# DMA scratch cut to 4 KB: three tiles for x, four band buffers from the first group on, eight of 16 blocks on GpSimd, weights loaded by SyncE

## The chip, the cores and the metric

One core of a Trainium2 chip. The metric is device time in microseconds of one execution, lower is better; a kernel's time is the median of its runs. TensorE (PE) multiplies, VectorE (DVE), ScalarE (ACT) and GpSimd (POOL) work on rows of up to 128 partitions, SyncE (SP) only issues DMAs. SBUF is one arena of 128 partitions that the kernel divides by hand.

## The reference

```
x: (16, 192, 32, 32) f32                       # B, C, H, W
w_sym = (w + rot90(w) + rot180(w) + rot270(w)) * 0.25      # w: (192, 1, 7, 7)
x = x + depthwise_conv7x7(layernorm_over_C(x, eps=1e-6), w_sym, pad=3)
t = tokens(x)                                  # (16, 1024, 192)
h = bitlinear(layernorm_over_C(t, eps=1e-5), W1, b1)       # 192 -> 768, sign weights in 5 groups of rows,
h = gelu(h)                                    #   then 8-bit absmax scaling in 5 groups of 3 images
t = t + bitlinear(h, W2, b2)                   # 768 -> 192, the same two steps
return t back as (16, 192, 32, 32)             # image 16 gets zero from bitlinear: x alone
```

## The kernel before, in words

The work has three stages; the change touches the first two and what prepares the third.

Stage one (to about 88 us) takes x in eight pairs of images. SyncE loads pair k in three DMAs (`load_x`, L310 to L314) into a tile `nat[k % 2]` of 12 KB per partition: one of the two tiles lies over the end of `X1` (the place of the last pair), the other at `R`, behind `XN`. TensorE transposes it in eight steps per pair (L958, L959, semaphore `tr1`), so that pixels are on partitions, ScalarE evicts each step into `X1` (`bring`, L469), VectorE takes statistics of it (`stats1`, L685, `merge`), ScalarE the square root (`deviation`, L475), VectorE the factors (`factors1`, L691 and L693, semaphore `nm`). The 16 blocks of a pair (4 image rows of one image each) are then normalised into `XN`, those in `VBLK` by VectorE (L700), the others by ScalarE (L482). `XN` holds channels outermost, so a block's 192 values are written 512 bytes apart.

Meanwhile VectorE builds the convolution's bands: it symmetrises the 7x7 kernels and writes them 32 times, shifted, into `KX`, a tile that was zeroed half by VectorE (L644) and half by GpSimd (L394). `KX` lies in the part of `X1` where pairs 2 to 5 go, so their evictions wait until SyncE has stored its four pieces to the DRAM tensor `kz_d` (L323), one piece ahead of the load of each of the pairs 2 to 5.

Stage two (to about 235 us) is the convolution as banded matrices: 48 groups of 4 channels, 24 matmuls each (L976, semaphore `conv`), after which VectorE adds the group's result to `X1` (L750, `cev`). A group's bands are four DMAs from `kz_d` of 112 KB, each for 32 partitions and with pieces of 896 bytes (`load_bands`, L296): SyncE issues two, ScalarE two (from group 2 on). The space between the bands must be zero; the loads write only the bands, so a buffer is zeroed once, by GpSimd (semaphore `blank`), before its first use. Buffer of group u is `BUFS[u]`: two buffers lie at `R` (behind the whole of stage one's tile), a third lies in `XN` and is used from group 5 (`THIRD`) on, when the channels under it are done, a fourth from group 26 (`FOURTH`). At group 24 (`conv` 24) GpSimd issues ten DMAs for the weights W1 (five of 51 partitions with 2304 bytes each, L409) and W2 (five of 38 partitions with 3072 bytes, L411) into places in `XN`; VectorE sums them from group 28 on, ScalarE takes their signs from group 38 on, TensorE transposes them.

Stage three is the two matrix products with their scaling, over half images; none of its code is changed. Its `normal` (L816 on VectorE, L426 on GpSimd) and GpSimd's `low` (L435) appear in rows below.

The order on each engine is the order in which its program is written; engines meet only at semaphores.

## Time and profile before

| | us |
|---|---|
| median of 3 runs (611.32, 613.7, 615.29) | 613.7 |
| profiled execution, its own time | 617.74 |
| its span, first to last instruction | 615.9 |
| TensorE busy in it | 496.8 (81%) |
| VectorE busy | 467.1 (76%) |
| ScalarE busy | 382.0 (62%) |
| GpSimd busy | 219.7 (36%) |

Busy times are sums over the whole span and say nothing of which engine a stage waits for; the rows below are cut by stage for that. The profile names engines PE, DVE, ACT, POOL, SP; a `q` behind the name is its queue of issued DMAs, and L976 is line 976 of the kernel. Text in brackets behind a timeline row is the idle time of the engine just before it and what ended that.

### The profile page before, as it was taken

What the parts mean: (1) busy time and instruction counts of PE and PEld (TensorE: products, weight loads), DVE (VectorE), ACT (ScalarE), POOL (GpSimd) and SP (SyncE); (2) the same over time, 40 slices, a digit from 0 to 9 for tenths busy, and PEclk for the clock granted to TensorE, in tenths of its full rate; (3) what the DMA queues carried; (4) which work ended last, traced back from release to release, by engine and by line L of the source; (5) the groups of instructions that cost most, each with busy time, mean ns of one, the idle gap of its engine ahead of it and who ended that gap; (6) DMA issues with size and microseconds to landing.
All of it is one profiled execution on the core that took longest, in us unless ns stands there. A gap on an engine that the chain in (4) does not pass through costs nothing.

```text
span 615.9 us, 9847 instructions
## 1 busy us (share of the span) xinstructions
PE 496.8 (81%) x3552; PEld 353.5 (57%) x3552; DVE 467.1 (76%) x1041; ACT 382.0 (62%) x598; POOL 219.7 (36%) x221
## 2 busy tenths in 40 slices
PE   2355527999969996758789989998999999987893
PEld 2255527999969995324335545555555555545562
DVE  7987861222228987996799898799989989699675
ACT  2688950000000353637799989998999898989550
POOL 4000000000400002212076747576666567558450
PEclk9666759999979997979999989999999999999798
DMA  8998325566965646940011000122222423263345
GB/s 223 290 316 248 104 61 150 149 175 169 204 161 150 178 124 250 386 157 1 27 51 53 27 27 0 52 82 74 78 74 77 133 78 101 80 230 104 125 135 178
DMA packets 55280, 81.29 MB, mean 132 GB/s; under 512 B 7361, under 2 KB 39105, under 8 KB 55232
## 3 DMA queue, kind: packets, MB, share of 16 engines
q1 hardware_dynamic: 39616, 68.28, 36.5%
q10 hardware_dynamic: 15136, 11.22, 6.5%
q0 software_dynamic: 480, 1.17, 0.9%
q8 instruction: 28, 0.46, 0.3%
q14 instruction: 20, 0.16, 0.1%
HBM read 53.12 MB, written 27.53 MB: 131 GB/s over the span
## 4 chain that ended last, share of the span: by engine, by line
PE 42%; DVE 22%; ACT 18%; DMA 10%; issue 5%; SPq 3%; ACTq 0%; DVEq 0%
PE bank L976 19%; DMA arena<-x 6%; PE bank L1058 5%; ACT arena L566 5%; DVE am L844 5%; ACT arena L560 4%; DMA arena<-kz_d 3%; PE bank L1026 3%; PE bank L1027 3%; PE bank L1028 3%; PE bank L1068 2%; DVE arena L816 2%; DVE arena L831 2%; ACT arena L482 2%; DVE arena L766 2%
## 5 line engine op out<-in xcount | busy, mean ns | idle before, releaser
L435 POOL TENSOR_TENSOR arena<-arena 128x512 f16<-128x512 f32 x159 | 186.9, 1212 | 120.6 <-DVE arena L831 99.3
L976 PE MATMUL bank<-arena 128*128 128x112 f32 (+1 forms) x1152 | 136.1, 283 | 20.8 <-ACT arena L482 12.6
L560 ACT ACTIVATE arena<-bank,b1s 128x512 f32<-128x512 f32 x180 | 125.1, 703 | 42.2 <-PE bank L1028 41.8
L976 PEld LDWEIGHTS bank<-arena 128*128 128x128 f32 x1152 | 135.0, 199 | 21.7 <-ACT arena L482 12.8
L1058 PE MATMUL bank<-arena 128*128 128x512 f16 x360 | 106.4, 390 | 5.4 <-ACT arena L584 3.6
L566 ACT ACTIVATE arena<-arena,gm 128x1024 f32<-128x1024 f32 x90 | 102.7, 1163 | 1.7 <-DVE gm L866 1.7
L844 DVE TENSOR_REDUCE am<-arena 128x1 f32<-128x3072 f32 x30 | 100.3, 3343 | 3.5 <-ACT arena L560 3.5
L750 DVE TENSOR_TENSOR arena<-bank,arena 128x512 f32<-128x512 f32 x48 | 33.2, 691 | 81.0 <-PE bank L976 80.9
L1026 PE MATMUL bank<-arena 128*128 128x512 f16 x180 | 71.0, 395 | 26.0 <-DVE arena L824 17.7
L497 ACT ACTIVATE arena<-arena,wmean 51x576 f16<-51x576 f32 (+1 forms) x10 | 8.6, 856 | 129.0 <-DVE wmean L724 116.2
L1027 PE MATMUL bank<-arena 128*128 128x512 f16 x180 | 70.6, 392 | 0.0
L1028 PE MATMUL bank<-arena 128*128 128x512 f16 x180 | 70.2, 390 | 0.0
L958 PE MATMUL bank<-identf,arena 128*128 128x128 f32 x128 | 33.4, 365 | 40.9 <-DMA arena<-x 40.9
L1058 PEld LDWEIGHTS bank<-arena 128*128 128x128 f16 x360 | 34.5, 99 | 47.7 <-issue 4.6
L426 POOL TENSOR_SCALAR arena<-arena,VR,SM 128x192 f32<-128x192 f32 x28 | 14.4, 526 | 108.8 <-DVE arena L816 75.7
L816 DVE TENSOR_SCALAR arena<-arena,VR,SM 128x192 f32<-128x192 f32 x92 | 44.1, 539 | 8.4 <-issue 8.2
L1026 PEld LDWEIGHTS bank<-arena 128*128 128x128 f16 x180 | 17.8, 99 | 56.6 <-DVE arena L824 21.3
L958 PEld LDWEIGHTS bank<-identf,arena 128*128 128x128 f32 x128 | 22.7, 194 | 42.8 <-DMA arena<-x 32.6
L831 DVE CAST arena<-arena 128x2048 f16<-128x2048 f32 (+1 forms) x30 | 35.8, 1195 | 13.6 <-ACT arena L566 11.9
L1068 PE MATMUL bank<-arena 128*64 128x256 f16 x720 | 46.1, 276 | 0.0
L1068 PEld LDWEIGHTS bank<-arena 128*64 128x64 f16 x720 | 37.5, 109 | 13.8 <-issue 13.4
L573 ACT ACTIVATE arena<-arena 128x1024 f16<-128x1024 f32 x37 | 39.7, 1072 | 1.7 <-PE bank L1068 1.7
(118 smaller groups left out, 684.9 us busy)
## 6 DMA issues: line engine op xcount, KB each, us to landing
arena<-park_d SPq DMA_DIRECT2D x44, 384.0 KB, 3.6
arena<-kz_d SPq DMA_DIRECT2D x100, 112.0 KB, 2.9
arena<-kz_d ACTq DMA_DIRECT2D x92, 112.0 KB, 3.4
park_d<-arena SPq DMA_DIRECT2D x6, 1536.0 KB, 14.5
arena<-x SPq DMA_DIRECT2D x8, 1024.0 KB, 8.9
out<-arena SPq DMA_DIRECT2D x32, 256.0 KB, 2.0
kz_d<-arena SPq DMA_DIRECT2D x8, 672.0 KB, 11.0
arena<-x SPq DMA_DIRECT2D x16, 256.0 KB, 9.8
```

The lines of the kernel that those rows point to most:

```text
L435: last = pool.tensor_tensor(out=low_half(u, m, m + 1), in0=yslot(u)[:, 2 * m:2 * m + 2, :], in1=hib(u, m, m + 1), op=ALU.subtract)
L560: act.activation(yslot(s)[:, 2 * m:2 * m + 2, :], m1p[c % 2][:, :].rearrange("p (h n) -> p h n", h=2), ACT.Identity, bias=b1s[:, m:m + 1], ...
L566: act.activation(y, y, ACT.Gelu, scale=gm[:, 5:6]).then_inc(gelu, 1)
L816: last = v.tensor_scalar(TN[:, h % 2, jj, :], x1[:, jj, :], VR[:, n:n + 1], SM[:, n:n + 1], ALU.mult, ALU.add)
L844: v.tensor_reduce(am[:, u % GT:u % GT + 1], yslot(u), AX.XY, ALU.max, apply_absolute_value=True).then_inc(amx, 1)
L958: t.transpose(o[:, b, 0:P], nat[k % 2][:, b, cols], identf[:, :])
L976: last = t.matmul(ps[:, :, lo:hi], WB[BUFS[g]][:, 1 - db, c, :], xn[:, :, lo + db:hi + db], start=(db == 0), stop=(db == -1))
L1026: t.matmul(o, W1A[:, fs], TT[:, s % 2, 0, :], start=True, stop=False)
L1027: t.matmul(o, W1M[:, fs], TT[:, s % 2, 1, :], start=False, stop=False)
L1028: t.matmul(o, W1Q[:, fs], TT[:, s % 2, 2, :], start=False, stop=True).then_inc(mm1, 1)
L1058: last = t.matmul(o, W2T[:, m, 0:P], src, start=(i == n == 0), stop=(i == MT - 1 and n == 1))
L1068: last = t.matmul(m2b[e * C1:(e + 1) * C1, 0:QTR], W2T[:, m, P:C], src[:, e, :], start=(m == n == 0), stop=(m == MT - 1 and n == 1))
```

## The change

The scratch that the program sets aside for DMAs described by software goes from its default of 16 KB to 4 KB of each partition; the arena grows by these 3072 words. They are used so:

- x has three tiles: two at `R`, one over the end of `X1`. Loads 0, 1 and 2 are issued at once, load k waits for the transposition of pair k-3. The pieces of `KX` are stored ahead of pairs 3 to 6.
- Four band buffers lie at `R`, over two tiles of x. GpSimd clears the first two once pair 6 is transposed and the last two once pair 7 is. Groups 0 to 3 are loaded whole by SyncE, later ones half by ScalarE.
- GpSimd normalises eight blocks of each pair (`GBLK`), VectorE two, ScalarE six; in the last pair it is four, six and six.
- The weights are loaded by SyncE, one DMA behind the band loads of each of the groups 16 to 25.
- `KX` is zeroed in three shares: the first half by VectorE before all else, the third quarter by ScalarE's copy of zeros, the last by GpSimd.
- `bring` is issued in two halves with `deviation` of the pair before between them, for every pair; VectorE calls `factors1` in the middle of `stats1`.

```diff
@@ -46,7 +46,7 @@
-ARENA = 52480
+ARENA = 55552
 YR, Y2R = 9, 8
...
@@ -56,7 +56,9 @@
-VBLK = {k: (0, 1, 2, 3, 8, 9, 10) if k < PAIRS - 2 else tuple(range(9)) for k in range(PAIRS)}
+VBLK = {k: (0, 8) if k < PAIRS - 1 else (0, 1, 2, 8, 9, 10) for k in range(PAIRS)}
+GBLK = {k: (1, 2, 3, 4, 9, 10, 11, 12) if k < PAIRS - 1 else (3, 4, 11, 12) for k in range(PAIRS)}
+NATS = 3
...
@@ -69,12 +71,8 @@
-THIRD, FOURTH = 5, 26
-BUFS = [(0, 1, 0, 1, 0, 2)[u] if u <= THIRD else (1, 0, 2)[u % 3] if u < FOURTH else (3, 2, 1, 0)[(u - FOURTH) % 4]
-        for u in range(NCG)]
-ROOM = {THIRD: 3, FOURTH: 23}
+BUFS = 4
+ROOM_W = (12, 17)
...
@@ -109,14 +107,13 @@
         PW = 3 * PIX
-        nat = [view(at, PW).rearrange("p (s n) -> p s n", s=3) for at in (XB - 2 * NB * C, R)]
+        nat = [view(at, PW).rearrange("p (s n) -> p s n", s=3) for at in (R, R + PW, XB - 2 * NB * C)]
...
-        spare = XB + WW + WTN + GROUPS * (3 * C + HID)
-        wb_at = [R, R + WW, XB, spare]
-        assert WW <= NN * CG * ROOM[THIRD] and spare + WW <= XB + NN * CG * ROOM[FOURTH]
+        assert 2 * WW == PW
+        wb_at = [R + i * WW for i in range(BUFS)]
         WF = [view(at, WW) for at in wb_at]
...
@@ -288,13 +280,13 @@
-            q.wait_ge(blank, 1 if u < THIRD else 2 if u < FOURTH else 3)
-            if user_before(u) >= 0:
-                q.wait_ge(conv, user_before(u) + 1)
+            q.wait_ge(blank, 1 if u % BUFS < 2 else 2)
+            if u >= BUFS:
+                q.wait_ge(conv, u - BUFS + 1)
             for r in rows:
-                dst = WF[BUFS[u]][r * W:(r + 1) * W].rearrange("p (c q) -> p c q", c=CG)
+                dst = WF[u % BUFS][r * W:(r + 1) * W].rearrange("p (c q) -> p c q", c=CG)
                 q.dma_start(dst[:, :, (r + 1) * W:(r + 1 + KS) * W], kz_d[u].rearrange("w (c q) -> w c q", c=CG)) \
-                    .then_inc(ld_wb[BUFS[u]], 16)
+                    .then_inc(ld_wb[u % BUFS], 16)
...
@@ -308,28 +300,36 @@
             def load_x(k):
-                t = nat[k % 2]
-                sp.dma_start(t[:, 0:2, :], x[2 * k:2 * k + 2, 0:P, :].rearrange("b c n -> c b n")).then_inc(ld_x[k % 2], 16)
+                t = nat[k % NATS]
+                sp.dma_start(t[:, 0:2, :], x[2 * k:2 * k + 2, 0:P, :].rearrange("b c n -> c b n")).then_inc(ld_x[k % NATS], 16)
                 for e in range(2):
-                    sp.dma_start(t[e * C1:(e + 1) * C1, 2, :], x[2 * k + e, P:C, :]).then_inc(ld_x[k % 2], 16)
-            load_x(0)
-            load_x(1)
-            for k in range(2, PAIRS):
-                i = k - 2
-                if i < W // KP:
-                    sp.wait_ge(ker_step, 8 + KP * (i + 1))
+                    sp.dma_start(t[e * C1:(e + 1) * C1, 2, :], x[2 * k + e, P:C, :]).then_inc(ld_x[k % NATS], 16)
+            for k in range(PAIRS):
+                i = k - NATS
+                if 0 <= i < W // KP:
+                    sp.wait_ge(ker_step, KER_HEAD + KP * (i + 1))
                     for h in range(2):
...
                             .then_inc(st_ker[i], 16)
-                sp.wait_ge(tr1, NB * (k - 1))
+                if k >= NATS:
+                    sp.wait_ge(tr1, NB * (k - NATS + 1))
                 load_x(k)
...
             for u in range(NCG):
-                load_bands(sp, u, range(RB) if u < 2 else range(RB // 2))
+                load_bands(sp, u, range(RB) if u < BUFS else range(RB // 2))
+                q = u - BUFS - ROOM_W[0]
+                if 0 <= q < GROUPS:
+                    sp.wait_ge(conv, ROOM_W[0] + q)
+                    sp.dma_start(w1w[0:RP1, q, :], w1[q * 3 * RP1:(q + 1) * 3 * RP1, :]
+                                 .rearrange("(p r) c -> p (r c)", r=3)).then_inc(ld_w, 16)
+                q = u - BUFS - ROOM_W[1]
+                if 0 <= q < GROUPS:
+                    sp.wait_ge(conv, ROOM_W[1] + q)
+                    sp.dma_start(w2w[0:RP2, q, :], w2[q * RP2:(q + 1) * RP2, :]).then_inc(ld_w, 16)
...
@@ -391,25 +391,35 @@
             pool.memset(eps[:, 1:2], 1e-5 / (XSC * XSC)).then_inc(consts, 1)
-            pool.memset(KX[:, W // 2:], 0.0).then_inc(zeroed, 1)
+            pool.memset(KX[:, 3 * W // 4:], 0.0).then_inc(zeroed, 1)
             pool.memset(ident, 0.0).then_inc(consts, 1)
...
             pool.memset(ones, 1.0).then_inc(consts, 1)
-            pool.wait_ge(tr1, NB * PAIRS)
-            for i in range(6):
-                last = pool.memset(view(R + i * WW // 3, WW // 3), 0.0)
-            last.then_inc(blank, 1)
-            pool.wait_ge(conv, ROOM[THIRD])
-            pool.memset(WF[2], 0.0).then_inc(blank, 1)
-            pool.wait_ge(conv, ROOM[FOURTH])
-            pool.memset(WF[3], 0.0).then_inc(blank, 1)
-            pool.wait_ge(conv, ROOM[FOURTH] + 1)
-            for q in range(GROUPS):
-                pool.dma_start(w1w[0:RP1, q, :], w1[q * 3 * RP1:(q + 1) * 3 * RP1, :]
-                               .rearrange("(p r) c -> p (r c)", r=3)).then_inc(ld_w, 16)
-                pool.dma_start(w2w[0:RP2, q, :], w2[q * RP2:(q + 1) * RP2, :]).then_inc(ld_w, 16)
+            def clear(k):
+                pool.wait_ge(tr1, NB * k)
+                for i in range(6):
+                    last = pool.memset(view(R + (k % 2 == 0) * PW + i * WW // 3, WW // 3), 0.0)
+                last.then_inc(blank, 1)
+            def normal1(k):
+                pool.wait_ge(nm, k + 1)
+                for n in GBLK[k]:
+                    b = 2 * NB * k + n
+                    last = pool.tensor_scalar(XN[:, :, b], X1[:, b, :], var1(k)[:, n:n + 1], mean1(k)[:, n:n + 1],
+                                              ALU.mult, ALU.add)
+                last.then_inc(xnG, 1)
+            for k in range(PAIRS):
+                if k == PAIRS - 2:
+                    clear(PAIRS - 1)
+                if k == PAIRS - 1:
+                    clear(PAIRS)
+                normal1(k)
+            pool.wait_ge(conv, ROOM_W[0])
             for m in (W1A, W1M, W1Q):
...
@@ -452,10 +462,12 @@
                 act.dma_start(b2s[e * C1:(e + 1) * C1, 1:2], b2[P:C].rearrange("(p o) -> p o", o=1)).then_inc(ld_b, 16)
+            act.wait_ge(zeroV, 1)
+            act.activation(KX[:, W // 2:3 * W // 4], KX[:, 0:W // 4], ACT.Copy).then_inc(zeroA, 1)
             act.wait_ge(consts, 4)
-            def bring(k):
-                for j in range(NB):
+            def bring(k, j0, j1):
+                for j in range(j0, j1):
                     t = NB * k + j
...
@@ -700,17 +713,12 @@
-            for k in range(PAIRS + 1):
-                if 0 < k < PAIRS - 1:
-                    factors1(k - 1)
+            for k in range(PAIRS):
+                stats1(k)
+                if k:
                     normal1(k - 1)
-                if k < PAIRS:
-                    stats1(k)
-                if k == PAIRS - 1:
-                    normal1(k - 1)
-                if k == PAIRS:
-                    factors1(k - 1)
-                    normal1(k - 1)
+            factors1(PAIRS - 1)
+            normal1(PAIRS - 1)
...
@@ -1142,7 +1151,7 @@
-    nc = bacc.Bacc("TRN2", target_bir_lowering=False, num_devices=1)
+    nc = bacc.Bacc("TRN2", target_bir_lowering=False, num_devices=1, dynamic_dma_scratch_size=4096)
     arrays, args = {}, []
```

## Rows read from the trace of the kernel before

**Rows 1.** Windows: busy time by engine, PEclk, DMA share, GB/s.

```profile
0.00:70.60 70.60, 29.70 (x169) 27.81 (x169) 58.39 (x230) 50.15 (x110) 7.36 (x12) 0.77 0.90 257
112.00:160.00 48.00, 48.00 (x432) 48.00 (x432) 12.20 (x19) 0.00 (x0) 1.38 (x1) 1.00 0.63 171
160.00:176.00 16.00, 11.04 (x97) 10.74 (x96) 3.40 (x5) 0.00 (x0) 5.49 (x14) 0.94 1.04 225
240.00:250.00 10.00, 7.54 (x32) 5.38 (x33) 6.59 (x38) 3.60 (x7) 3.90 (x8) 0.55 1.02 394
```

**Rows 2.** Waits of SyncE's queue, 0 to 90 us: total, times, longest.

```profile
SPq L312 <- PE bank L959: 27.2, 5, 8.2
```

**Rows 3.** TensorE's timeline: start, length in us; idle before.

```profile
10.22 0.66 PE L958 MATMUL bank<-identf,arena 128*128 128x128 f32 x2 [10.22 <-DMA arena<-x]
...
70.56 0.69 PE L958 MATMUL bank<-identf,arena 128*128 128x128 f32 x2 [4.70 <-DMA arena<-x]
...
88.14 7.45 PE L976 MATMUL bank<-arena 128*128 128x128 f32 x48 [12.61 <-ACT arena L482]
97.04 5.61 PE L976 MATMUL bank<-arena 128*128 128x128 f32 x48 [1.44 <-DMA arena<-kz_d]
104.45 63.49 PE L976 MATMUL bank<-arena 128*128 128x128 f32 x552 [1.80 <-DMA arena<-kz_d]
```

**Rows 4.** VectorE's timeline, the additions behind groups 0, 4, 26, 28, 47.

```profile
92.95 0.69 DVE L750 TENSOR_TENSOR arena<-bank,arena 128x512 f32<-128x512 f32 x1 [5.63 <-PE bank L976]
...
108.80 0.69 DVE L750 TENSOR_TENSOR arena<-bank,arena 128x512 f32<-128x512 f32 x1 [5.42 <-PE bank L976]
...
167.98 0.69 DVE L750 TENSOR_TENSOR arena<-bank,arena 128x512 f32<-128x512 f32 x1 [1.99 <-PE bank L976]
...
181.12 0.69 DVE L750 TENSOR_TENSOR arena<-bank,arena 128x512 f32<-128x512 f32 x1 [9.22 <-PE bank L976]
...
234.90 0.69 DVE L750 TENSOR_TENSOR arena<-bank,arena 128x512 f32<-128x512 f32 x1 [0.36 <-PE bank L976]
```

**Rows 5.** The chain that ended last, two of its transfers.

```profile
93.71 3.28 DMA arena<-kz_d
...
163.25 12.42 DMA arena<-kz_d
```

**Rows 6.** The page: a DMA queue, and an issue group.

```profile
q0 software_dynamic: 480, 1.17, 0.9%
...
arena<-w POOLq DMA_DIRECT2D x5, 114.8 KB, 6.5
```

**Rows 7.** ScalarE's and VectorE's timelines in stage one.

```profile
21.95 0.17 DVE L693 TENSOR_TENSOR SM<-SM,VR 128x16 f32<-128x16 f32 x1
...
74.58 3.22 ACT L469 ACTIVATE arena<-bank 128x384 f32<-128x384 f32 x8
77.59 0.41 ACT L475 ACTIVATE VR<-VR,eps 128x16 f32<-128x16 f32 x1
...
84.50 3.59 ACT L482 ACTIVATE arena<-arena,SM,VR 128x192 f32<-128x192 f32 x7 [2.32 <-DVE SM L693]
...
84.50 2.82 DVE L700 TENSOR_SCALAR arena<-arena,VR,SM 128x192 f32<-128x192 f32 x9
```

**Rows 8.** GpSimd's timeline: clearing, blocks of 192, subtractions of 512.

```profile
75.59 2.86 POOL L401 MEMSET arena<- 128x512 f32 x6 [67.31 <-PE bank L959]
...
241.40 1.95 POOL L426 TENSOR_SCALAR arena<-arena,VR,SM 128x192 f32<-128x192 f32 x4 [75.69 <-DVE arena L816]
...
310.49 6.78 POOL L435 TENSOR_TENSOR arena<-arena 128x512 f16<-128x512 f32 x6 [21.66 <-DVE arena L831]
```

**Rows 9.** VectorE's timeline: four blocks without and with GpSimd beside.

```profile
303.34 1.25 DVE L816 TENSOR_SCALAR arena<-arena,VR,SM 128x192 f32<-128x192 f32 x4
...
314.90 3.05 DVE L816 TENSOR_SCALAR arena<-arena,VR,SM 128x192 f32<-128x192 f32 x4
```

**Rows 10.** One line's instructions: ns min/median/max of a band issue.

```profile
L296 SPq DMA_DIRECT2D arena<-kz_d x100: 538/598/1657, 78.5 to 223.8; - x100
```

More of the change, by code:

```diff
@@ L131, in build @@
         assert at + GROUPS * HID <= XB + 6 * BLK
+        assert at <= XB + ROOM_W[0] * NN * CG
+        assert all(at + (q + 1) * HID <= XB + (ROOM_W[1] + q) * NN * CG for q in range(GROUPS))
         w1s = [w1w[:, g, 0:3 * C // 2].bitcast(F16).rearrange("p (r c) -> p r c", r=3) for g in range(GROUPS)]
@@ L159, in build @@
         at = ARENA - P - P // 2
-        assert YB + YC * MT * HALF <= at and R + PW <= at and R + 2 * WW <= at
+        assert YB + YC * MT * HALF <= at and R + 2 * PW <= at and R + BUFS * WW <= at
         ones, ident = view(at, P), view(at + P, P // 2, F16)
@@ L197, in build @@
         st_ker = [sem(f"st_ker{i}") for i in range(W // KP)]
-        ld_x = [sem(f"ld_x{i}") for i in range(2)]
+        ld_x = [sem(f"ld_x{i}") for i in range(NATS)]
         tr1 = sem("tr1"); ev_x = sem("ev_x")
@@ L259, in conv_out_parts @@
             return X1[:, :, g * CG:(g + 1) * CG], cps[g % 4][:, :].rearrange("p (c n) -> p n c", c=CG)
-        def uses(u):
-            return BUFS[:u + 1].count(BUFS[u])
-        def user_before(u):
-            return max((k for k in range(u) if BUFS[k] == BUFS[u]), default=-1)
         def mean1(k):
@@ L273, in var1 @@
             return VR[:, 2 * NB * (k % 3):2 * NB * (k % 3 + 1)]
-        KER_STEPS = 8 + W + 1
+        KER_HEAD = 7
+        KER_STEPS = KER_HEAD + W + 1
         def unit_pieces(k):
@@ L479, in normal1 @@
                 for n in range(2 * NB):
-                    if n not in VBLK[k]:
+                    if n not in VBLK[k] and n not in GBLK[k]:
                         b = 2 * NB * k + n
@@ L486, in _ @@
             for k in range(PAIRS + 1):
-                if k == PAIRS - 1:
-                    bring(k)
+                if k < PAIRS:
+                    bring(k, 0, NB // 2)
                 if k:
                     deviation(k - 1)
-                if k < PAIRS - 1:
-                    bring(k)
+                if k < PAIRS:
+                    bring(k, NB // 2, NB)
                 if k:
@@ L508, in _ @@
                 act.wait_ge(done, 32)
-            for g in range(2, NCG):
+            for g in range(BUFS, NCG):
                 load_bands(act, g, range(RB // 2, RB))
@@ L625, in _ @@
             v = nc.vector
+            v.memset(KX[:, 0:W // 2], 0.0).then_inc(zeroV, 1)
             dve.wait_ge(ld_k, 32)
@@ L643, in _ @@
             v.tensor_scalar(kacc, kacc, 0.25, None, ALU.mult).then_inc(ker_step, 1)
-            v.memset(KX[:, 0:W // 2], 0.0).then_inc(ker_step, 1)
-            dve.wait_ge(ker_step, 8)
+            dve.wait_ge(ker_step, KER_HEAD)
+            dve.wait_ge(zeroV, 1)
+            dve.wait_ge(zeroA, 1)
             for w in range(W):
-                if w == W // 2:
+                if w == 3 * W // 4:
                     dve.wait_ge(zeroed, 1)
@@ L678, in stats1 @@
                     dve.wait_ge(xnV, k - 2)
+                    dve.wait_ge(xnG, k - 2)
                 for j in range(NB):
-                    if k == PAIRS - 1 and j == NB // 2:
+                    if k and j == NB // 2:
                         factors1(k - 1)
@@ L949, in _ @@
             for k in range(PAIRS):
-                pe.wait_ge(ld_x[k % 2], 48 * (k // 2 + 1))
+                pe.wait_ge(ld_x[k % NATS], 48 * (k // NATS + 1))
                 for j in range(NB):
@@ L975, in conv_group @@
                         lo, hi = max(0, -db), min(NB, NB - db)
-                        last = t.matmul(ps[:, :, lo:hi], WB[BUFS[g]][:, 1 - db, c, :], xn[:, :, lo + db:hi + db],
+                        last = t.matmul(ps[:, :, lo:hi], WB[g % BUFS][:, 1 - db, c, :], xn[:, :, lo + db:hi + db],
                                         start=(db == 0), stop=(db == -1))
```

12 lines of the change are left out of this document (5 added, 7 removed).

## The prediction

> **What bounds the kernel now.** I read the windows first, to part the span into stages, then TensorE's timeline for what ended each of its idle times, then SyncE's waits, the chain, and VectorE's timeline for the rhythm of the convolution groups. The change touches the first two stages, up to 235 us.
>
> Stage one loads x, turns it over, computes the norm's factors and writes normalised blocks. The window from 0 to 70.6 [rows 1] gives in its last three figures the granted clock, the busy share of the DMA engines and the rate: they are 0.90 busy at 257 GB/s, while VectorE is busy for 58 of 70.6 us and ScalarE for 50. The bytes of x and of the kernel's bands set the pace. They don't quite fill it: SyncE stood 27.2 us, in five waits, before an x load because the tile it overwrites was not yet turned over [rows 2]. The last pair starts on TensorE at 70.56, released by the DMA [rows 3], and the first convolution matmul follows at 88.14, released by ScalarE's last normalised block. This tail is 17.6 us.
>
> Stage two is 48 convolution groups of 24 matmuls. VectorE adds each group's result right after it, so its starts are a clock of the groups [rows 4]: from group 4 (108.80) to group 26 (167.98) lie 22 groups in 59.18 us, 2.69 each, and undisturbed ones come every 2.68. Against that rhythm three intervals stick out. The first to the fifth group took 15.85 us for 4 groups, 5.13 too much, with TensorE waiting for bands at 97.04 and 104.45 [rows 3]; the chain has 3.28 us of DMA there [rows 5]. Groups 27 and 28 took 13.14 us for two, 7.78 too much; the chain shows why, a single band transfer of 12.42 us [rows 5] in the time when the weights come in by GpSimd's queue (480 packets, 0.9% of 16 engines' span [rows 6]) and the DMA share reads 1.04 against 0.63 in quiet groups [rows 1]. The last 19 groups took 53.78, 2.86 more than 19 x 2.68; that is the weights' sums and transposes, which stay.
>
> **Third tile for x.** With three tiles the load of pair k waits for pair k-3 instead of k-2, and three pairs are queued before anything is computed. Total DMA work stays: 0.90 x 70.6 = 63.5 us of all engines. Queued without gaps from about 2.5 us on (an estimate: the first pair is on TensorE at 10.22 [rows 3]) it ends at 66; as windows of pure transfer show shares slightly over one (1.02 at 240 to 250 [rows 1]), up to 4 us of these may be overlap counted twice, so 64 to 66. I take 65 for the last pair's landing in place of 70.56: 5.6 us earlier. What could come late next is the compute of one pair. ScalarE has 8 evictions (3.22), the square root (0.41) and now 6 blocks rather than 9, at 3.59/7 = 0.51 each, 3.1 [rows 7]: 6.7 us, below the 63.5/8 = 7.9 that a pair costs in DMA. The band stores are moved behind one more load each, and the evictions of pairs 2 to 5 wait for them since they overwrite the bands' tile; a store lands some 3 us after the pair it now follows, inside the 7.9. The zeroing of that tile in three shares (VectorE first, ScalarE by a copy, GpSimd half of its part) shortens nothing on the path: most lies under the first load, which TensorE has at 10.22 [rows 3]. ScalarE's copy of 3584 words starts near 7 and, at no more than 1.05 ns each by its evictions of 384 (3.22/8 [rows 7]), ends near 11 to 12, about where the first evictions begin in any case. I cost it at nothing; if that cover were missing it would be 1 us.
>
> **GpSimd takes eight blocks.** From the last pair's landing to its last eviction passed 77.8 - 70.56 = 7.2 us before, part of it spent on pair 5's nine blocks [rows 3, 7]; now ScalarE has 3.22 of evictions, 0.41 of root between their halves and some 2.5 left of pair 5's blocks, so they end near 65 + 6.1 = 71.1. Then ScalarE: 6 blocks of pair 6 (3.1), square root (0.4), VectorE's factors (0.5), 6 blocks of pair 7 (3.1): 78.2. VectorE: nine blocks took 2.82 [rows 7], six take 1.9, and end before that. GpSimd has the longest list. It gets pair 6's factors near 70.2, does eight blocks at 1.95/4 = 0.49 [rows 8], 3.9, then clears the second pair of band buffers, 2.86 [rows 8], then does four blocks, 1.95: 78.9. Two prices are unseen. One is that its blocks are now written with a stride of 512 bytes, where the traced ones are contiguous. ScalarE's pace per block doesn't tell, since it has no contiguous block of this size. I bound it from 0.49 to the 1.13 that its 512-element operations took (6.78/6 [rows 8]), and take 0.52, near the row with the same elements and operation (79.3 then). At the upper end the twelve last blocks cost 7.7 us more. The other is VectorE and GpSimd beside one another.
>
> Here the row speaks first: four of VectorE's blocks take 1.25 us alone and 3.05 with GpSimd's operations beside them, while the latter keep their 1.13 [rows 8, 9]; VectorE waits 0.45 us a block. The Trainium skill's "SBUF — State Buffer", section "Who interferes with whom", has this as an exclusive lock between GpSimd and VectorE's two-port operations, held for a whole instruction. By that rule, the trace agrees, VectorE's six last blocks could each wait.
>
> By the rows, 6 x 0.45 = 2.7 us takes VectorE's end to about 79.5, next to GpSimd's. With some waiting of both I take 79.8 for the first convolution matmul; before, it was 88.14. **Gain of stage one: 8.3 us.** The ends: 10, with x landed at 64 and no waiting; 5, with x at 66 and GpSimd's block at 0.7 us.
>
> **Four band buffers from the start.** A group's bands are asked for when its buffer is free. From conv 0's end to the start of group 2 passed 97.04 - 92.95 = 4.1 us [rows 3, 4]; with four buffers a load has three groups, 8.0 us, so 3.9 us are spare (with three it was 1.3). SyncE issues all 16 band loads of the first four groups itself at 0.60 each [rows 10]. The last eight wait for the second clearing, about 77, are issued by 82 and landed by 85; group 2 needs its half near 87.3 (79.8 plus a cold group of 4.8 and one of 2.7), group 3 at 90. So the 5.13 go, and the 0.22 behind them. Removed waits make nothing else late: VectorE's addition takes 0.69 of 2.68.
>
> **Weights by SyncE.** Ten loads, one per group from 16 to 25, instead of ten at once. Their wait on the convolution has passed already when the band load ahead of each has been let through, so nothing new is queued behind a wait; each adds one issue (0.6) to SyncE's 1.2 per group, within 2.68. In bytes they are 0.9% x 616 = 5.5 us of 16 engines, 0.55 a group; the group's own DMA share is 0.63 x 2.68 = 1.69, together 2.24 of 2.68. If spread like this the 7.78 vanish. The trace has no such load on SyncE's queue, so the price lies between 0 (a gain is excluded: the bytes have to move) and, worked out under the second rival, 22 us; I take 1.5, within 0 to 4 as long as all engines share them, because 3.9 us are spare and because mixing them cost 7.78 when all came at once and 1.3 was spare. **Gain of stage two: 5.13 + 0.22 + 7.78 - 1.5 = 11.6.**
>
> **Sum.** 8.3 + 11.6 = 19.9 us off a span of 615.9, which makes 596.0; the profiled execution itself was 617.74, so 597.8. It lay 4.0 above the median of 613.7, and against that I forecast **593.8**. Everything after 235 us keeps its order.
>
> **The rivals.** (a) *The forecast*, chance 0.56. Its range: stage one 5 to 10, stage two 9 to 13.1, so 590.6 to 600, and 3 lower for the spread of the runs shown (4 us among three).
>
> (b) *The weights crowd a few engines*, 0.28. A load of 51 or 38 rows may not be cut over 16 engines as band loads of 32 rows by four are. Were it 3 engines for the first kind and 2 for the second, each would carry 38 and 57 KB (115 KB a load [rows 6]). At the best rate in the trace, 394 GB/s over 16 engines at 1.02 [rows 1], that is 1.6 and 2.4 us beside 1.69 of bands; over 2.68 these engines fall behind by 0.6 a group and then 1.4, 10 us in all, of which 3.9 are spare: a stall of 6. At the rate of GpSimd's packets (1.17 MB in 88.7 us of engine time [rows 6], 13.2 KB per us) it is 2.9 and 4.3, 26 less 3.9: 22. Near the best rate is likelier, as these rows are long, and the stall of 6 to 10 gives 613.7 - 21.4 + 6 to 10 = 598 to 602; the far end gives 614. For it speaks that the mixing at 160 was so dear; against it that half of the group's time is spare.
>
> The Trainium skill's "DMA: Bandwidth & Descriptors", section "Why a DMA increments its semaphore by 16 and not by 1", says that a load from SyncE or ScalarE runs on the largest number of engines up to 16 that divides the slowest dimension, which is 3 for 51 and 2 for 38, and always on the lowest-numbered ones. No row of this trace shows such a load. By the rule this rival is the result, by the spread assumed above it is 593.8.
>
> (c) *GpSimd sets the pace: slower than before*, 0.04. It now carries 60 blocks and two clearings (5.7 us) from the first factors at 22.1 [rows 7] on: the convolution then starts at 22.1 + 5.7 + 60t. With 13.1 us won in stage two the kernel gets slower once this passes 101.2, at t = 1.22 us a block, and by 1% at 1.33. Its 512-element operations take 1.13, so 192 strided elements would have to cost more than 512 do there. At t = 0.75 it is not the pace, but the last twelve blocks add 3.1: 597, inside the range.
>
> (d) *The third tile brings nothing*, 0.08: if the DMA rate falls as queues deepen, x still lands at 70.5 and only the shorter tail (2.8) stays: 613.7 - 2.8 - 11.6 = 599.3.
>
> (e) *The change doesn't keep bands ahead*, 0.04: with all 16 first band loads on one queue group 2 or 3 still waits, as at 104.45 before; up to 5 of the 11.6 go: 599.
>
> **How the numbers follow.** All cases but (c) and the far end of (b) are faster by over 1%, which is about what a measurement of this kernel can tell from no change: 0.93. Within 1% lie the far end of (b) and half of (c): 0.05; slower 0.02. The range takes in (a), (d), (e) and most of (b): 587 to 603.
>
> **What would show it.** The last pair's first transposition near 65 (not 70.5); SyncE's wait before x loads well under 27 us; GpSimd's blocks about 0.5 us each and VectorE's waits beside them; first convolution matmul near 80; the first additions 2.68 apart with no wait for bands; no band transfer of over 6 us while the weights come, which else proves (b) by waits that sit in groups 16 to 28. The prediction is wrong if GpSimd's block is over 0.8 us, if x's rate falls, or if the weights' loads take longer than about 6 us to land.

## The result, and the profile after

The changed kernel takes 606.66 us (median of 16 runs, 603.34 to 613.55). The kernel before, run beside it, takes 615.57 (16 runs). The ratio of the two is 0.9846, interval 0.9819 to 0.9874, which makes it 9.5 us less (the two medians differ by 8.9). I had forecast 19.9 less, 593.8 with an upper end of 603, counted from the 613.7 of three runs. The profiled execution took 604.19, its span is 602.4.

The page no longer shows GpSimd's DMA queue of [rows 6]. Two windows of stage one and three of stage two (columns as in [rows 1]; the last takes in all the waits shown further down):

```profile
10.00:60.00 50.00, 28.55 (x158) 26.85 (x159) 44.56 (x190) 39.65 (x89) 24.14 (x40) 0.75 1.03 322
60.00:70.00 10.00, 5.21 (x36) 4.86 (x34) 9.21 (x37) 9.55 (x23) 8.38 (x16) 0.84 0.04 15
90.00:118.00 28.00, 28.00 (x254) 28.00 (x252) 6.92 (x10) 0.00 (x0) 0.20 (x4) 1.00 0.65 174
120.00:150.00 30.00, 26.11 (x229) 25.61 (x228) 6.91 (x10) 0.00 (x0) 0.00 (x0) 1.00 0.64 180
139.00:165.00 26.00, 18.28 (x154) 17.39 (x153) 4.15 (x6) 0.00 (x0) 0.00 (x0) 1.00 0.52 148
```

From 10 to 60 the DMA engines are busy without a gap, at 322 GB/s, and from 60 to 70 they rest (0.04; the share is 0.20 from 60 to 62 and 0 after). So x is in by about 61, and TensorE takes up the last pair at 62.23, right behind pair 6 and without a wait, not at 70.56. SyncE's wait for a free tile, 27.2 us before [rows 2], is now

```profile
SPq L304 <- PE bank L967: 4.3, 4, 2.0
```

TensorE's timeline (compare [rows 3]):

```profile
57.06 0.69 PE L966 MATMUL bank<-identf,arena 128*128 128x128 f32 x2 [5.04 <-DMA arena<-x]
...
80.20 59.63 PE L985 MATMUL bank<-arena 128*128 128x128 f32 x504 [14.99 <-POOL arena L411]
140.75 2.90 PE L985 MATMUL bank<-arena 128*128 128x128 f32 x24 [0.92 <-DMA arena<-kz_d]
145.30 2.90 PE L985 MATMUL bank<-arena 128*128 128x128 f32 x24 [1.65 <-DMA arena<-kz_d]
149.53 2.90 PE L985 MATMUL bank<-arena 128*128 128x128 f32 x24 [1.33 <-DMA arena<-kz_d]
153.57 2.90 PE L985 MATMUL bank<-arena 128*128 128x128 f32 x24 [1.14 <-DMA arena<-kz_d]
157.79 2.90 PE L985 MATMUL bank<-arena 128*128 128x128 f32 x24 [1.31 <-DMA arena<-kz_d]
162.06 21.66 PE L985 MATMUL bank<-arena 128*128 128x128 f32 x192 [1.37 <-DMA arena<-kz_d]
```

The first convolution matmul comes at 80.20, where I had it at 79.8. From there 504 matmuls, 21 groups, run without a stop, so the waits at 97.04 and 104.45 are gone. Then come six waits for bands in a row, of 0.92 to 1.65 us. VectorE's additions show what they cost (compare [rows 4]); these are the ones behind groups 0, 19, 26 and 47:

```profile
85.67 0.69 DVE L758 TENSOR_TENSOR arena<-bank,arena 128x512 f32<-128x512 f32 x1 [7.80 <-PE bank L985]
...
137.06 0.69 DVE L758 TENSOR_TENSOR arena<-bank,arena 128x512 f32<-128x512 f32 x1 [1.99 <-PE bank L985]
...
165.00 0.69 DVE L758 TENSOR_TENSOR arena<-bank,arena 128x512 f32<-128x512 f32 x1 [3.58 <-PE bank L985]
...
224.15 0.69 DVE L758 TENSOR_TENSOR arena<-bank,arena 128x512 f32<-128x512 f32 x1 [0.36 <-PE bank L985]
```

Between 137.06 and 165.00 lie 7 groups in 27.94 us, 9.18 more than 7 x 2.68. From there to group 47 pass 59.15 us for 21 groups, 2.87 too much, as before. The chain shows the cause as [rows 5] did, in two band transfers, and SyncE's queue shows what stood ahead of them:

```profile
135.02 10.14 DMA arena<-kz_d
...
148.93 13.00 DMA arena<-kz_d
```

```profile
130.29 0.46 SPq L327 DMA_DIRECT2D arena<-w  x1
131.74 1.18 SPq L288 DMA_DIRECT2D arena<-kz_d  x2
132.97 0.44 SPq L332 DMA_DIRECT2D arena<-w  x1
134.42 1.18 SPq L288 DMA_DIRECT2D arena<-kz_d  x2
135.65 0.44 SPq L332 DMA_DIRECT2D arena<-w  x1
```

These two band transfers last 10.14 and 13.00 us, where 2.8 (SyncE) and 3.3 (ScalarE) are the medians, while the mean DMA share from 120 to 150 is 0.64, no more than in the quiet groups before (0.65). The engines have time to spare in the mean, and yet single transfers are late. That is what rival (b) would look like.

The last addition comes at 224.15, against 234.90 [rows 4]: 10.75 us earlier. What follows it, stage three, takes 378 us in this trace and 381 in that of the kernel before; in the traces below, with the same stage three, it takes 379 to 384, so this difference says nothing.

### The profile page after: what moved, and what is told of

The parts are those of the page before. It is cut to its first block, busy times and chain, and to the rows that moved or that the text cites. A ratio compares the mean times of both kernels' runs of the same rounds, so it can differ in the third digit from the quotient of the medians.

```text
span 602.4 us, 9858 instructions
## 1 busy us (share of the span) xinstructions
PE 490.2 (81%) x3552; PEld 349.6 (58%) x3552; DVE 458.2 (76%) x1001; ACT 374.8 (62%) x579; POOL 247.6 (41%) x275
## 4 chain that ended last, share of the span: by engine, by line
PE 39%; DVE 22%; ACT 14%; DMA 13%; issue 5%; SPq 3%; POOL 2%; DVEq 0%; ACTq 0%
PE bank L985 19%; DMA arena<-x 7%; DVE am L852 5%; PE bank L1067 5%; ACT arena L576 5%; ACT arena L570 4%; DMA arena<-kz_d 4%; DVE arena L824 3%; DVE arena L839 3%; DVE arena L774 3%; DMA arena<-park_d 3%; PE bank L1077 2%; PE bank L1035 2%; PE bank L1037 2%; PE bank L1036 2%
## 5 line engine op out<-in xcount | busy, mean ns | idle before, releaser
L985 PE MATMUL bank<-arena 128*128 128x112 f32 (+1 forms) x1152 | 133.8, 279 | 22.7 <-POOL arena L411 15.0
L985 PEld LDWEIGHTS bank<-arena 128*128 128x128 f32 x1152 | 132.4, 196 | 23.9 <-issue 15.2
L1067 PE MATMUL bank<-arena 128*128 128x512 f16 x360 | 104.6, 385 | 3.9 <-ACT arena L594 2.7
L1035 PE MATMUL bank<-arena 128*128 128x512 f16 x180 | 70.3, 391 | 28.5 <-DVE arena L832 20.0
L436 POOL TENSOR_SCALAR arena<-arena,VR,SM 128x192 f32<-128x192 f32 x28 | 14.1, 517 | 148.4 <-DVE arena L824 114.8
L1037 PE MATMUL bank<-arena 128*128 128x512 f16 x180 | 69.7, 387 | 0.0
L1036 PE MATMUL bank<-arena 128*128 128x512 f16 x180 | 69.7, 387 | 0.0
L411 POOL TENSOR_SCALAR arena<-arena,VR,SM 128x192 f32<-128x192 f32 x60 | 36.0, 696 | 32.2 <-DVE SM L706 32.1
L839 DVE CAST arena<-arena 128x2048 f16<-128x2048 f32 (+1 forms) x30 | 35.3, 1176 | 14.6 <-ACT arena L576 11.6
```

The source lines that it names most:

```text
L985: last = t.matmul(ps[:, :, lo:hi], WB[g % BUFS][:, 1 - db, c, :], xn[:, :, lo + db:hi + db], start=(db == 0), stop=(db == -1))
L1035: t.matmul(o, W1A[:, fs], TT[:, s % 2, 0, :], start=True, stop=False)
L1036: t.matmul(o, W1M[:, fs], TT[:, s % 2, 1, :], start=False, stop=False)
L1037: t.matmul(o, W1Q[:, fs], TT[:, s % 2, 2, :], start=False, stop=True).then_inc(mm1, 1)
L1067: last = t.matmul(o, W2T[:, m, 0:P], src, start=(i == n == 0), stop=(i == MT - 1 and n == 1))
```

## The experiments

Two theories on the six waits. **F**: a weight load of 51 or 38 rows runs on 3 or 2 engines, which can't keep up with it and the bands. **Q**: the weights' bytes and issues in SyncE's queue delay the band loads behind them, whatever their shape. "Excess" is the time between two of VectorE's additions beyond 2.68 us a group; of the whole convolution it is the time from the first addition to the last less 47 x 2.68.

**1. The same bytes in other shapes.** In `a1_spread` each load is cut in two:

```diff
-   sp.dma_start(w1w[0:RP1, q, :], w1[q * 3 * RP1:(q + 1) * 3 * RP1, :] ...).then_inc(ld_w, 16)
+   for a, z in ((0, 48), (48, 51)):
+       sp.dma_start(w1w[a:z, q, :], w1[q * 3 * RP1 + 3 * a:q * 3 * RP1 + 3 * z, :] ...).then_inc(ld_w, 16)
...
-   sp.dma_start(w2w[0:RP2, q, :], w2[q * RP2:(q + 1) * RP2, :]).then_inc(ld_w, 16)
+   for a, z in ((0, 32), (32, 38)):
+       sp.dma_start(w2w[a:z, q, :], w2[q * RP2 + a:q * RP2 + z, :]).then_inc(ld_w, 16)
...
-   dve.wait_ge(ld_w, 32 * GROUPS)
+   dve.wait_ge(ld_w, 64 * GROUPS)
```

> Each weight load is cut in two along the partitions: 51 rows into 48 and 3, 38 rows into 32 and 6. Same bytes, same places in SyncE's queue, ten issues more. Theory F (a load of 51 or 38 rows runs on 3 or 2 of the 16 engines, which fall behind with the bands): nearly all bytes now go over 16 engines, so the 9.2 us by which groups 21 to 26 of the changed kernel exceed 2.68 each shrink to under 2; the last addition comes about 7 to 9 us earlier, counted from the first one, and the time is near 598. Rival Q (it is the weights' bytes and issues in SyncE's queue, ahead of the next band loads, whatever their shape): ten more issues make it the same or worse, 9 to 13 us of excess, time 606 to 610.

In `a2_one_engine` the cuts are (0, 17), (17, 34), (34, 51) and (0, 19), (19, 38).

> The dose the other way: 51 rows as three loads of 17, 38 rows as two of 19, again the same bytes. Theory F with the rule that the engines' number must divide the rows and is at most 16: 17 and 19 rows leave one engine, always the lowest, so its 115 KB a group take about 5 us beside 1.7 of bands in 2.68 us: 4 us behind a group, for ten groups 40, less 4 spare: the excess of groups 17 to 28 is 30 to 40 us, time near 635. If the number of engines doesn't go by division, or rival Q holds: excess 9 to 13 us, time 606 to 610.

Measured: `a1_spread` took 595.26 us (6 runs), ratio to the kernel before 0.9669, interval 0.9632 to 0.9707. `a2_one_engine` took 629.05 in its one execution (635 expected). A window of the spread kernel, its TensorE timeline, and that of `a2_one_engine` with one window:

```profile
120.00:150.00 30.00, 30.00 (x272) 30.00 (x270) 8.08 (x12) 0.00 (x0) 0.00 (x0) 1.00 0.76 212
```

```profile
80.32 93.29 PE L987 MATMUL bank<-arena 128*128 128x128 f32 x816 [14.69 <-DVE arena L715]
174.96 0.39 PE L995 MATMUL bank<-wsum,arena 128*128 128x10 f32 x2 [1.35 <-DVE wsum L728]
```

```profile
129.52 2.90 PE L987 MATMUL bank<-arena 128*128 128x128 f32 x24 [1.81 <-DMA arena<-kz_d]
136.40 4.43 PE L987 MATMUL bank<-arena 128*128 128x128 f32 x24 [3.97 <-DMA arena<-kz_d]
142.39 2.90 PE L987 MATMUL bank<-arena 128*128 128x128 f32 x24 [1.56 <-DMA arena<-kz_d]
148.59 4.29 PE L987 MATMUL bank<-arena 128*128 128x128 f32 x24 [3.30 <-DMA arena<-kz_d]
...
136.00:141.00 5.00, 4.43 (x24) 4.29 (x24) 0.13 (x1) 0.00 (x0) 0.00 (x0) 0.66 0.22 67
```

In the spread kernel 34 groups run without one wait from 80.32 to 173.6, with more issues and a higher DMA share (0.76, against 0.64), and the excess is 2.87: just the sums and transposes of the weights. In `a2_one_engine` the excess is 37.28; less 2.86 for those and 0.26 at the start, the weights cost 34.2 us, where F had 30 to 40. Theory Q is out: with the same bytes the cost is 9.2 us for 10 loads, 0 for 20 and 34.2 for 25, so it follows neither bytes nor issues but the rows of a load.

Not all of the 34.2 is time of the transfers themselves. In `a2_one_engine` SyncE's issues get long too: the issue of a band load takes up to 3.51 us there (median 0.65), up to 1.08 in the changed kernel, and the chain runs through them. So that the size came out as expected is in part luck.

The Trainium skill's "DMA: Bandwidth & Descriptors", section "Why a DMA increments its semaphore by 16 and not by 1", has the number of engines as the largest up to 16 that divides the rows: 16 for 48 and 32, 3 for 51, 2 for 38, 1 for 17 and 19. The three outcomes follow that order. The traces don't name the engine of a packet, but they keep each packet's time and size, and between 100 and 200 us the weights' packets are the only ones of 2304 and 3072 bytes. Counted from these, of the time in which any of them is under way:

| loads of | most at once | share of the time with no more than |
|---|---|---|
| 51 rows | 6 | three: 0.94 |
| 38 rows | 3 | two: 0.99 |
| 17 and 19 rows | 2 | one: 0.98 |
| 48 and 3 rows | 14 | three: 0.41 |
| 32 and 6 rows | 12 | two: 0.37 |

That fits 3, 2, 1 and up to 16 engines, and the trace agrees with the page. The few packets beyond three beside loads of 51 rows can come from two such loads in flight together; that was not taken apart. A load of 38 rows takes 3.5 to 4.0 us from its first packet to the end of its last, longer than the 2.68 of a group, while one is issued in every group.

**2. GpSimd's queue again, and one buffer fewer.** `a3_gpsimd_weights` takes the ten loads out of SyncE's program and puts them back on GpSimd, behind a wait for group 24, as in the kernel before. `a4_three_buffers` changes one line:

```diff
-BUFS = 4
+BUFS = 3
```

> The weights are loaded by GpSimd again, all ten at once after group 24 as in the kernel before, all else as changed. The kernel before lost 7.78 us there with three buffers, which leave a band load 1.3 us spare; four leave 3.9. If that loss is a delay of the bands that the spare time absorbs: 7.78 - 2.6, an excess of about 5 us, time 4 us below the changed kernel, near 602.5. If it is a loss of DMA throughput that no buffer absorbs: 7 to 8 us, time near 605.

> Three band buffers instead of four from the start, all else as changed. By my account a band load needs 4.1 us and three buffers give it 5.4: no stall at the start, 1.3 us spare; with the weights on few engines (theory F) the backlog has 2.6 us less to hide in, so their excess grows from 9.2 to about 11.8. If the stalls have nothing to do with how far ahead the bands are asked for, it stays 9.2.

Measured: `a3_gpsimd_weights` took 601.71 us (4 runs), ratio 0.9785, interval 0.9743 to 0.9826. It has one wait for bands; the two lines above it here are those of the kernel before in the same place:

```profile
168.27 2.90 PE L976 MATMUL bank<-arena 128*128 128x128 f32 x24 [0.32 <-DMA arena<-kz_d]
175.81 18.67 PE L976 MATMUL bank<-arena 128*128 128x128 f32 x144 [4.64 <-DMA arena<-kz_d]
...
160.28 17.93 PE L980 MATMUL bank<-arena 128*128 128x128 f32 x144 [2.55 <-DMA arena<-kz_d]
```

One interval is long, by 4.40. The kernel before lost 7.78 in the same place. The waits went from 4.96 to 2.55, by 2.4 us, close to the 2.6 of spare time that the fourth buffer adds: the loss was a delay of the bands. The rest of both losses is mostly a slow clock, which the prediction didn't see. In the kernel before the granted clock is 0.50 (1.2 GHz) from 174 to 180, and the group that starts at 175.81 has its addition 5.31 us later, where 2.94 is usual after a short wait; here the clock is 0.50 from 162 to 164, and 4.57 us pass.

This run holds a second lesson. With the same four buffers the loads cost 4.40 on GpSimd's queue and 9.18 on SyncE's, and the time is 601.71 against 606.66 (the intervals of the two ratios just touch; in the traces the difference is 4.8 to 6.2). Without that move the change would have done better: as it was written, the move of the loads to SyncE made the kernel some 5 us slower.

`a4_three_buffers` took 611.14 in one execution. From group 15 to 25 its excess adds up to 11.76, against 9.18 with four, and 11.8 expected. That it fits so well is chance, since four traces with four buffers and the same loads have 9.2, 9.3, 10.2 and 10.6. Three more intervals are long, by 1.23 (group 7), 0.33 (28) and 0.41 (38), which the four buffers don't have: 1.3 us of spare time is not always enough even where no weights come. At the start three buffers have no wait either. What removed the 5.13 there is that the third one is ready at once.

**3. What stage one gained from.** `a5_two_tiles` has `NATS = 2` and is otherwise the changed kernel. `a6_no_gpsimd_blocks` has `GBLK` empty and the `VBLK` of the kernel before (and no `xnG`).

> The changed kernel with two tiles for x, so that load k waits for pair k-2 again and the band stores come one load earlier. If the third tile is what brought x in by 60 us instead of 70.6: gaps in the DMA are back, the last pair lands at 67 to 71 and the convolution starts at 84 to 87 (some 17 us after the landing). If x came early for another reason (the earlier band stores, the shorter pairs on ScalarE): landing 60 to 63, start 80 to 81.

> The changed kernel with GpSimd's blocks given back: VectorE and ScalarE normalise seven and nine of 16 as in the kernel before, and nine and seven in the last two pairs; three tiles and four buffers stay. Theory (with x landing early, ScalarE's work per pair, 3.3 of evictions, 0.3 of root and 3.1 of blocks, is what the pace then hangs on): with nine blocks it is 8.1 us a pair, eight pairs from 11.5 on, so the convolution starts near 84 to 86, and taking GpSimd in was worth about 5 us. Rival (GpSimd's list is itself the end of stage one and costs as much as it saves): 79 to 81.

Measured, one execution each: 611.25 and 603.17 us. Their TensorE timelines, with the last start of a pair that waited for x (pair 7 with two tiles, pair 6 with three), and the first convolution matmul:

```profile
68.11 0.69 PE L966 MATMUL bank<-identf,arena 128*128 128x128 f32 x2 [4.91 <-DMA arena<-x]
...
85.11 5.22 PE L985 MATMUL bank<-arena 128*128 128x128 f32 x23 [11.61 <-DVE arena L713]
```

```profile
57.00 0.69 PE L964 MATMUL bank<-identf,arena 128*128 128x128 f32 x2 [4.75 <-DMA arena<-x]
...
79.99 10.20 PE L982 MATMUL bank<-arena 128*128 128x128 f32 x76 [14.81 <-ACT arena L491]
```

Two tiles put the last pair's x back to 68.11 and the start to 85.11: the third tile is worth 4.9 us in these two traces, and 3.4 to 6.0 if all six traces with the changed kernel's own stage one are taken, which start between 79.14 and 81.67. GpSimd's share, which I had held worth 5 us, is worth nothing: 79.99 without, 80.20 with. Where it goes is seen from the last factors on. In the changed kernel they are ready at 73.84, and then:

```profile
69.13 4.80 POOL L411 TENSOR_SCALAR arena<-arena,VR,SM 128x192 f32<-128x192 f32 x8
73.79 3.88 POOL L404 MEMSET arena<- 128x512 f32 x6
77.66 2.33 POOL L411 TENSOR_SCALAR arena<-arena,VR,SM 128x192 f32<-128x192 f32 x4
```

```profile
72.11 0.57 DVE L685 TENSOR_SCALAR SM<-SM 128x16 f32<-128x16 f32 x1
...
73.88 3.98 DVE L713 TENSOR_SCALAR arena<-arena,VR,SM 128x192 f32<-128x192 f32 x6
```

VectorE's six blocks take 3.98 us, 0.66 each, beside GpSimd's clearing, and the clearing takes 3.88 beside them, where it took 2.86 alone [rows 8]. Even a scaling of 16 columns (L685) takes 0.57 here beside GpSimd's blocks, 0.17 in the kernel before. So from the last factors to the convolution pass 6.4 us. Without GpSimd's blocks the factors come at 76.32, 2.5 us later, but after them

```profile
76.36 2.82 DVE L711 TENSOR_SCALAR arena<-arena,VR,SM 128x192 f32<-128x192 f32 x9
```

nine blocks take 2.82, and 3.7 us pass. The gain in the middle is paid back at the end. The middle's gain is small since ScalarE was never back to back, as I had reckoned with 8.1 us a pair: from 20 us on to pair 6, at 57, the pairs came some 9 us apart by x's DMA, and even nine blocks on ScalarE fitted between.

**4. Versions.** All but `b0_changed_again`, which is the changed kernel itself, have the spread loads. `a7_clear_last` moves `clear(PAIRS)` behind GpSimd's last blocks.

> The spread weight loads, and GpSimd clears the second pair of band buffers after its last four blocks instead of before them. Theory (GpSimd's list is the end of stage one: eight blocks 4.8, clearing 3.9, four blocks 2.3 in the changed kernel's trace, and TensorE is released by them): the clearing leaves the path, GpSimd ends near 76, VectorE's six blocks near 77.9, so the first convolution matmul comes at 77.5 to 78.5 instead of 80.2, time 2 us below the spread kernel, near 593. The bands of groups 2 and 3 are then asked for some 1.5 us later and needed at 86: no new wait. Rival (ScalarE and VectorE end as late as GpSimd in any case, or groups 2 and 3 now wait for bands): no gain, 595 or more.

Measured: 596.2 us (6 runs), ratio 0.967, interval 0.9634 to 0.9705, no different from the spread kernel's. The start is at 80.78, released by VectorE:

```profile
74.61 6.06 DVE L714 TENSOR_SCALAR arena<-arena,VR,SM 128x192 f32<-128x192 f32 x6
```

```profile
69.87 7.54 POOL L413 TENSOR_SCALAR arena<-arena,VR,SM 128x192 f32<-128x192 f32 x12
77.22 2.93 POOL L406 MEMSET arena<- 128x512 f32 x6
```

GpSimd's list did get shorter, but VectorE's six blocks now take 6.06 us, 1.01 each, with GpSimd's blocks beside them. The expectation rested on the 3.98 of one trace, and the clearing beside them doesn't ensure that. The spread kernel's own trace, with the clearing in its old place, has

```profile
73.93 6.29 DVE L715 TENSOR_SCALAR arena<-arena,VR,SM 128x192 f32<-128x192 f32 x6
```

```profile
74.40 2.90 POOL L406 MEMSET arena<- 128x512 f32 x6
```

and the start at 80.32 is released by VectorE there too. Seven traces have these last blocks and this clearing. In five (3.98 or 3.99) the clearing starts 0.1 us before VectorE's blocks; in two, this one and that of `a5_two_tiles` (6.29), it starts 0.47 after them and keeps its 2.9. So either both engines lose, or VectorE alone loses more, and the start comes out the same. That the order of the two starts decides it fits all seven traces, but was not tested by itself. Taking work off GpSimd's list doesn't help as long as what is left runs beside VectorE.

The next three versions were run together with the changed kernel on the same chip. `b1_spread_no_gpsimd_blocks` joins the spread loads with the edit of `a6_no_gpsimd_blocks`. The core of `b2_last_pair_two_engines`, and what `b3_clear_after_vector` adds to it (with nine blocks on VectorE and seven on ScalarE):

```diff
-VBLK = {k: (0, 8) if k < PAIRS - 1 else (0, 1, 2, 8, 9, 10) for k in range(PAIRS)}
-GBLK = {k: (1, 2, 3, 4, 9, 10, 11, 12) if k < PAIRS - 1 else (3, 4, 11, 12) for k in range(PAIRS)}
+VBLK = {k: (0, 8) if k < PAIRS - 1 else (0, 1, 2, 3, 8, 9, 10) for k in range(PAIRS)}
+GBLK = {k: (1, 2, 3, 4, 9, 10, 11, 12) if k < PAIRS - 1 else () for k in range(PAIRS)}
...
                 if k == PAIRS - 1:
+                    pool.wait_ge(xnV, PAIRS)
                     clear(PAIRS)
```

> The changed kernel itself, unaltered, for a time on the same chip as the next three: both theories expect 604 to 608, a first convolution matmul at 79 to 81 and an excess of groups 20 to 26 near 9.

> Spread weight loads, and no blocks on GpSimd at all. The look at the changed kernel without GpSimd's blocks gave a start of the convolution at 79.99 against 80.20. Theory (GpSimd's share buys nothing: what it takes off ScalarE and VectorE comes back as VectorE's waits beside it and as its own list at the end): time that of the spread kernel, 594 to 597, start at 79 to 81. Rival (that look was chance and the share is worth the 5 us that I had expected of it): 600, start at 85.

> Spread weight loads; GpSimd keeps its eight blocks in pairs 0 to 6 but has none in the last pair, where ScalarE does nine (4.6 us) and VectorE seven. GpSimd clears meanwhile, so VectorE waits beside it, about 0.65 us a block. Theory (each instruction of VectorE beside one of GpSimd waits it out): from the last factors at 73.9 VectorE ends near 78.4 and ScalarE near 78.5, start at 78.6, 1.6 us earlier than 80.2. Rival (the start hangs on something before the last factors): 80.

> As the last one, but the second clearing waits until VectorE has done its blocks of the last pair, now nine, and ScalarE does seven: GpSimd stands still beside them. Theory: VectorE's nine take 2.8 us again as in the kernel before, ScalarE's seven 3.6, start at 77.6, 2.6 us earlier than 80.2; the clearing ends near 79.7 and the bands of group 2 land near 85, just ahead of their use, so no new wait or one under 1 us; time near 593. If VectorE's blocks still take over 5 us, it is not GpSimd that slows them, and the start stays at 80.

| kernel | us, median of 6 | ratio to the kernel before | interval | last factors to start | start of convolution |
|---|---|---|---|---|---|
| b0_changed_again | 608.02 | 0.988 | 0.9847 to 0.9913 | 6.3 | 81.67 |
| b1_spread_no_gpsimd_blocks | 595.6 | 0.9697 | 0.9669 to 0.9726 | 3.7 | 79.87 |
| b2_last_pair_two_engines | 593.52 | 0.966 | 0.9631 to 0.9689 | 4.6 | 78.30 |
| b3_clear_after_vector | 594.14 | 0.9658 | 0.9618 to 0.9699 | 3.7 | 80.70 |

In `b0_changed_again` the start, 81.67, and the excess of groups 20 to 26, 10.6, lie above what was expected (79 to 81, near 9). So a start differs by 2 us from one trace of the same stage one to the next, and the column of times from the last factors to the start is the steadier measure of what b2 and b3 change. The first fence is of b2, the other two of b3:

```profile
56.87 0.69 PE L969 MATMUL bank<-identf,arena 128*128 128x128 f32 x2 [4.61 <-DMA arena<-x]
...
78.30 31.93 PE L988 MATMUL bank<-arena 128*128 128x128 f32 x264 [13.26 <-ACT arena L495]
```

```profile
77.06 3.16 DVE L717 TENSOR_SCALAR arena<-arena,VR,SM 128x192 f32<-128x192 f32 x9
```

```profile
60.77 0.69 PE L970 MATMUL bank<-identf,arena 128*128 128x128 f32 x2 [6.05 <-DMA arena<-x]
...
80.70 10.39 PE L989 MATMUL bank<-arena 128*128 128x128 f32 x72 [12.68 <-ACT arena L496]
91.80 18.47 PE L989 MATMUL bank<-arena 128*128 128x128 f32 x163 [0.71 <-DMA arena<-kz_d]
```

The step that b2 changes did what was expected (start at 78.6 expected, 78.30 measured; 4.6 us from the factors on, where b0 has 6.3). The b3 profile is of its longest execution (600.25 us, median 594.14), with x 4 us late (60.77), so its start says nothing. What can be read in it is the step itself: nine blocks take 3.16 us with GpSimd still, and 3.7 pass from the factors to the start. This trace also has new waits for bands, 1.35 us in groups 2 and 3; whether the shorter executions have them isn't shown. By time the plain spread kernel, a7, b1, b2 and b3 can't be told apart (their intervals overlap), and all five beat both kernels of this case. b1 shows that this result is had without GpSimd's blocks, so with less of a change.

## Why the prediction was wrong

**The step that failed is the size taken for "Weights by SyncE".** I put 1.5 us, within 0 to 4, on condition that all engines share the loads; 9.18 was measured (10.6 in the second trace of the changed kernel), since loads of 51 and 38 rows go over few engines, 3 and 2 by their packets. The mechanism was on paper as rival (b), at 0.28, with a stall of 6 to 10 at the likelier rate: 9.2 lies inside. The reason for holding the rival unlikely, that half of a group's DMA time is spare, is a mean over 16 engines and doesn't bear on a load that uses 2; the windows after show the mean share at 0.64 while TensorE waits. I ranked the rival low although the page of the Trainium skill that the prediction cites gave its numbers of engines and no row spoke against it. With this term right the forecast is 601.5, against 604.2 (613.7 less the 9.5 measured); of the 2.7 between them the terms below explain 1.5. With the loads spread, the forecast without the term is 592.3, a gain of 21.4 us; by its ratio `a1_spread` gained 20.4.

**Third tile for x**: right in kind (4.9 us by `a5_two_tiles`), off in both halves of its sum. x landed by about 61, not 65, since the queue kept full moved 322 GB/s over 50 us, where 257 at a share of 0.90 had made me count on 286. But pair 6 had come only at 57.06 and pair 7 right behind it, and ScalarE, with pair 5's blocks still to do, evicted pair 6 until 62.97 and pair 7 until 69.2. The tail from x to the convolution grew from 17.6 to some 19 us instead of falling to 14.8. The two errors cancel to 0.4 us, at 80.20 against 79.8, which is luck. SyncE's wait fell to 4.3 as said.

**GpSimd takes eight blocks**: the block took 0.60 us (4.80/8), between the bounds of 0.49 and 1.13 and near the 0.52 taken; that a strided write costs more is the likely reason, not shown apart. VectorE's waits beside it were priced at 0.45 a block; they were 0.35 in the changed kernel's trace (0.66 less the 0.31 of nine in 2.82) and 0.70 to 0.74 where the six took 6.06 and 6.29. What I missed is that GpSimd's clearing can get slower too, by 1.0, and that the sum of it all is no gain: `a6_no_gpsimd_blocks` and `b1_spread_no_gpsimd_blocks` start the convolution as early.

**Four buffers**: right. The 5.13 and 0.22 are gone and no wait took their place. (The 7.78 of the kernel before was a wait for bands of 4.96, and most of the rest the slow clock behind it; both go with the wait.) Not foreseen was the start. In windows of 2 us the granted clock is 0.50 (1.2 GHz) from the first matmul at 80.20 to 86 and 0.87 from 86 to 88; in the kernel before it is 0.50 from 88.14 to 92 and 0.99 from 92 to 94. The first group takes 5.47 instead of 4.81 us and the second 3.15 instead of 2.68, 1.1 more in all. TensorE had stood idle for 15.0 us ahead of it, 12.6 before, but the length of that doesn't explain it: the first group takes 5.47 after 11.6 us idle in `a5_two_tiles` and 4.37 after 14.85 in `a7_clear_last`. The cause stays open.

**Rivals**: (b) is what happened. (c) was far, GpSimd's block would have had to cost twice its 0.60. (d) is refuted by `a5_two_tiles` and by the 322 GB/s, (e) by 21 groups without a wait.

**The sum by terms**, in the traces: the first addition comes at 85.67 instead of 92.95, 7.28 us gained, and the groups from it on gain 3.47, together 10.75, where 19.9 was forecast. Of the missing 9.15 the weights' loads are 7.7, the slow clock in the first two groups 1.1 and the later start 0.4. The medians and the ratio put the gain at 8.9 to 9.5.

## What to carry to other kernels

Before moving a load from one queue to another, look at its number of rows: the mean DMA share can stand at 0.64 while one transfer takes 13 us, and cutting loads of 51 and 38 rows into 48 and 3 and into 32 and 6 was worth 11 us here. A third engine for elementwise work is worth what remains after the waits it causes; look at the stretch behind the last producer, where VectorE's six blocks cost 1.9 us alone (by nine in 2.82) and 4.0 to 6.3 beside GpSimd. And when a sum comes out right to 0.4 us, check its terms: two of mine were off by some 4 us each.

## What the runs showed of the hardware

- Equal bytes in equal places of SyncE's queue cost nothing as loads of 48 and 32 rows (with rests of 3 and 6), 9.2 to 10.6 us as loads of 51 and 38, and 34.2 us as loads of 17 and 19. The packets under way at once are mostly no more than 3, 2 and 1 for loads of 51, 38 and 17 or 19 rows, and up to 14 for the spread ones.
- Beside GpSimd's operations VectorE's block of 192 elements takes 0.62 to 1.05 us instead of 0.31 (seven in 4.31 in b2, six in 6.29 in `a1_spread`). GpSimd's clearing takes 3.88 instead of 2.86 where VectorE's six take 3.98, and keeps 2.90 where they take 6.29; GpSimd's blocks take 0.58 to 0.63 throughout. VectorE's statistics show next to nothing of it (L698, eight in 2.17 us at 68.95, beside GpSimd's blocks; L685 of the kernel before, eight in 2.17 at 78.41, alone).
- Six waits of 0.9 to 1.7 us with 2.9 us of matmuls between them left the granted clock at 1.00 in the window from 139 to 165. With waits of 3.3 and 4.0 us ahead of a group, in `a2_one_engine`, the group itself took 4.3 to 4.4 instead of 2.9 us, and the window of 136 to 141 around one of them has 0.66. The wait of 2.55 us in `a3_gpsimd_weights` and that of 4.64 in the kernel before were followed by stretches at 0.50.
- Loads of x and stores of bands together, queued without a gap, moved 322 GB/s at a share of 1.03 over 50 us; the kernel before, with gaps, made it 257 at 0.90 over its first 70.6.
